# Minus mu as three rows of the score product instead of the sigmoid's bias operand

## What is computed

```python
def _L1_attn_ref(sequence, ln_gamma, ln_beta, Wq, bq, Wk, bk, Wv, bv, Wo, bo, mu):
    ...
    q = _split_heads(x @ Wq.T + bq)
    k = _split_heads(x @ Wk.T + bk)
    v = _split_heads(x @ Wv.T + bv)
    scale = HEAD_DIM ** 0.5
    scores = jnp.einsum('bhqd,bhkd->bhqk', q, k) / scale
    scores = jax.nn.sigmoid(scores - mu) * jnp.exp(scores)
    scores = scores / jnp.sum(scores, axis=-1, keepdims=True)
    out = jnp.einsum('bhqk,bhkd->bhqd', scores, v)
    ...
```

## Time and profile before

| what | value |
|---|---|
| median of 3 runs | 737.53 us |
| the profiled execution, its own time | 736.84 us |
| span in its profile | 735.0 us |
| PE busy | 680.0 us, 93% |
| DVE busy | 459.6 us, 63% |
| ACT busy | 350.2 us, 48% |
| POOL busy | 142.8 us, 19% |
| sigmoid activations (L944) | 64, 67.7 us |
| exp activations of the second attention (L943) | 64, 61.7 us |
| mean granted clock of PE | 0.976 |

### The profile page before, as it was taken

How to read it: one execution, slowest core, us unless ns; L and a number is a source line. 1 busy time by engine, 2 the same in 40 slices (tenths; PEclk the granted TensorE clock), 3 DMA queues, 4 the chain that set the end, 5 groups by cost and what they waited for, 6 DMA issues and landing times.

```text
span 735.0 us, 15948 instructions
## 1 busy us (share of the span) xinstructions
PE 680.0 (93%) x5563; PEld 541.1 (74%) x5563; DVE 459.6 (63%) x1177; ACT 350.2 (48%) x604; POOL 142.8 (19%) x183
## 2 busy tenths in 40 slices
PE   5789999999989999999999999998899999998855
PEld 4668877877768988977878799997576666765433
DVE  3758787887664453256632332333589999978786
ACT  2354455346425211222122212221998999999745
POOL 3010131232223130000000022200434555211000
PEclk9999999999999999999999999999999999999975
DMA  6868133223437466656465657552432244212003
GB/s 175 232 186 250 38 95 102 86 72 86 132 122 248 152 223 231 224 187 218 144 260 195 216 188 230 173 194 58 122 86 61 85 116 115 77 40 58 1 15 101
DMA packets 70311, 102.80 MB, mean 140 GB/s; under 512 B 8400, under 2 KB 57816, under 8 KB 70112
## 3 DMA queue, kind: packets, MB, share of 16 engines
q1 hardware_dynamic: 66848, 93.41, 40.7%
q0 software_dynamic: 3136, 8.40, 3.7%
q10 hardware_dynamic: 256, 0.07, 0.0%
HBM read 64.41 MB, written 12.19 MB: 104 GB/s over the span
## 4 chain that ended last, share of the span: by engine, by line
PE 68%; DVE 16%; issue 5%; ACT 5%; DMA 2%; POOL 1%; DVEq 1%; ACTq 0%; SPq 0%; POOLq 0%
PE psum L2356 17%; PE psum L2303 15%; DVE arena L1487 5%; PE psum L1969 4%; PE psum L2247 3%; PE psum L2261 3%; PE psum L2232 3%; PE psum L2238 2%; PE psum L2293 2%; DVE arena L1342 2%; PE psum L1993 2%; PE psum L1977 1%; PE psum L2331 1%; PE psum L2031 1%; ACT arena L944 1%
## 5 line engine op out<-in xcount | busy, mean ns | idle before, releaser
L2356 PE MATMUL psum<-arena 128*128 (+1 forms) x576 | 130.7, 380 | 1.9 <-DVE arena L1671 1.4
L2303 PE MATMUL psum<-arena 128*128 128x128 f32 x1024 | 120.5, 276 | 1.1 <-issue 1.0
L2303 PEld LDWEIGHTS psum<-arena 128*128 128x128 f32 x1024 | 118.1, 192 | 4.1 <-issue 3.2
L2356 PEld LDWEIGHTS psum<-arena 128*128 128x128 f32 (+1 forms) x576 | 103.2, 184 | 18.8 <-issue 3.2
L978 ACT ACTIVATE arena<-psum,arena 128x128 f32<-128x128 f32 x128 | 36.5, 368 | 148.6 <-DVE arena L1645 106.9
L2247 PE MATMUL psum<-arena 96*128 96x256 bf16 x512 | 74.0, 274 | 6.1 <-ACT arena L943 5.1
L1487 DVE TENSOR_TENSOR arena<-arena 128x1024 f32<-128x1024 f32 x64 | 77.7, 1284 | 0.8 <-ACT arena L943 0.8
L1671 DVE TENSOR_TENSOR arena<-psum,arena 128x256 f32<-128x256 f32 (+1 forms) x40 | 17.0, 424 | 97.7 <-PE psum L2356 80.9
L2247 PEld LDWEIGHTS psum<-arena 96*128 96x128 bf16 x512 | 44.0, 97 | 37.7 <-ACT arena L943 12.3
L944 ACT ACTIVATE arena<-psum,neg_mu 128x1024 f32<-128x1024 f32 x64 | 67.7, 1118 | 3.7 <-PE psum L2247 3.5
L943 ACT ACTIVATE arena<-psum 128x1024 f32<-128x1024 f32 x64 | 61.7, 1036 | 12.9 <-DVE arena L1671 8.5
(11 more groups left out here) (355 smaller groups left out, 1277.9 us busy)
## 6 DMA issues: line engine op xcount, KB each, us to landing
arena<-in_L_ffn_w_dram SPq DMA_DIRECT2D x48, 1024.0 KB, 5.4
arena<-arena SPq DMA_DIRECT2D x192, 128.0 KB, 2.4
yg<-arena SPq DMA_DIRECT2D x36, 128.0 KB, 1.7
arena<-xg SPq DMA_DIRECT2D x32, 128.0 KB, 2.1
out_dram<-arena SPq DMA_DIRECT2D x8, 256.0 KB, 2.1
xg<-zeros SPq DMA_DIRECT2D x9, 128.0 KB, 2.9
arena<-in_x_dram SPq DMA_DIRECT2D x8, 128.0 KB, 2.2
arena<-in_L_ffn_b_dram SPq DMA_DIRECT2D x1, 1024.0 KB, 14.0
```

Source lines behind the costliest of these rows:

```text
L2303: mm = pe.matmul(psum[:, 2 * v + c // HALF, (c % HALF) * P:(c % HALF + 1) * P], w1[:, d, c * P:(c + 1) * P], xtT[:, v, d, :], start=(d == ...
L2356: mm = pe.matmul(y_bank[0:rows], hidT[:, u, c, 0:rows], w2s[:, one(e), c, :].rearrange("p o n -> p (o n)"), start=(c == 0), stop=(c == HC ...
```

## The change

`scores` gets its number of rows as an argument: 96 in the pass of exp, MU_ROWS = 99 in the pass of sigmoid. The three added rows are ones in `stackq1` and, in `stackk1`, three bf16 parts of minus mu, so that the product comes out as s - mu. ACT's sigmoid has no bias operand any more. The rows are filled once:

- DVE, after tile i = 18: eight small instructions, each waited for, split `neg_mu` into three bf16 parts and put part n into partition 96 + n of a column (`mu_part`).
- POOL, between `scale1(1)` and `gather(2)`: a memset of ones and a copy of the column, spread over 4096 elements, both on 3 partitions; a wait at the end for the copy.
- SP, behind the unit loop: two DMAs copy the rows from the stacks of parity 0 to those of parity 1.
- PE waits for the fill before its first pass and for the two DMAs at batch 1.

`scale1` also lost an argument: both its uses now count on one semaphore.

```diff
+MU_ROWS = ROWS + 3
...
+        MU_STEPS, MU_TILE = W8_STEPS + 8, 18
...
+                sp.wait_ge(S["l1_hi"], UNITS)
+                sp.wait_ge(S["set_done"], 5)
+                for stack in (stackq1, stackk1):
+                    sp.dma_start(stack[1][ROWS:MU_ROWS].rearrange("d h t -> d (h t)"),
+                                 stack[0][ROWS:MU_ROWS].rearrange("d h t -> d (h t)")).then_inc(S["mu_in"], 16)
...
+                def shift_rows():
+
+                    pool.wait_ge(S["l1_hi"], SPARE_UNTIL)
+                    pool.wait_ge(S["n_rstd"], 2)
+                    pool.memset(stackq1[0][ROWS:MU_ROWS], 1.0).then_inc(S["set_done"], 1)
+                    pool.wait_ge(S["l2_mm"], SPARE_UNTIL)
+                    pool.wait_ge(S["w8_step"], MU_STEPS)
+                    pool.wait_ge(S["set_done"], 4)
+                    pool.tensor_copy(stackk1[0][ROWS:MU_ROWS].rearrange("p h t -> p (h t)"),
+                                     mu_part[ROWS:MU_ROWS, :].to_broadcast([MU_ROWS - ROWS, HEADS * T])).then_inc(S["set_done"], 1)
+                    pool.wait_ge(S["set_done"], 5)
+
                 for b in range(3):
+                    if b == 2:
+                        shift_rows()
                     gather(b)
...
-                    return act.activation(out, in_, ACT.Sigmoid, bias=neg_mu[:])
+                    return act.activation(out, in_, ACT.Sigmoid)
...
+                def shift_parts():
+
+                    dve.wait_ge(S["wT_done"], WT_STEPS + 3)
+                    chain(dve.tensor_copy(mu_split[:, 0:1], neg_mu[:]))
+                    chain(dve.tensor_tensor(mu_rest[:, 0:1], neg_mu[:], mu_split[:, 0:1], ALU.subtract))
+                    chain(dve.tensor_copy(mu_split[:, 1:2], mu_rest[:, 0:1]))
+                    chain(dve.tensor_tensor(mu_rest[:, 1:2], mu_rest[:, 0:1], mu_split[:, 1:2], ALU.subtract))
+                    chain(dve.tensor_copy(mu_split[:, 2:3], mu_rest[:, 1:2]))
+                    chain(dve.tensor_tensor(mu_part[:], mu_split[:, 0:1], ident[:, ROWS:ROWS + 1], ALU.mult))
+                    for n in range(1, 3):
+                        chain(dve.scalar_tensor_tensor(out=mu_part[:], in0=mu_split[:, n:n + 1], scalar=ident[:, ROWS + n:ROWS + n + 1],
+                                                       in1=mu_part[:], op0=ALU.mult, op1=ALU.add))
...
+                    if i == MU_TILE:
+                        shift_parts()
...
                             if b == 0 and p == 0:
-                                pe.wait_ge(S["set_done"], 3)
+                                pe.wait_ge(S["set_done"], 5)
+                            if b == 1 and p == 0:
+                                pe.wait_ge(S["mu_in"], 2 * 16)
...
-                            scores(b, u, p, S["s1_mm"])
+                            scores(b, u, p, ROWS if u == 0 else MU_ROWS, S["s1_mm"])
...
-                            scores(b, u, p, S["s2_mm"])
+                            scores(b, u, p, MU_ROWS if u == 0 else ROWS, S["s2_mm"])
```

More of the change, by code:

```diff
@@ L203, in tower_kernel @@
         neg_mu = sb("neg_mu", [P, 1], F32)
+        mu_rest = sb("mu_rest", [P, 2], F32)
+        mu_split = sb("mu_split", [P, 3], BF16)
+        mu_part = sb("mu_part", [P, 1], F32)
         ones_row = sb("ones_row", [1, P], F32)
@@ L422, in tower_kernel @@
             s1_mm f1_done s2_mm f2_done prodD n_pv n_oa n_ot1 n_rr n_on n_ot2 n_oT n_wo n_hbo n_h3
-            m_stat m_mv m_eps m_rstd x3_done am_done
+            m_stat m_mv mu_in m_rstd x3_done am_done
             w8_in w8_step w8_mm w8_done q_step am_mm f_y f_ed qz_q fT_mm fT_done f_mm f_o f_back f_out""".split()
@@ L782, in _, with scale1 @@
                 batches(pool, iteration, B + 2)
-                def scale1(b, n, got, s_eps, s_rstd):
+                eps_steps = [0]
+                def scale1(b, n, got, s_rstd):
                     pool.wait_ge(got, QT * (b + 1))
@@ L788, in scale1 @@
                     scale, shift = (1.0 + LN1_EPS, LN_EPS * LN1_EPS) if n == 0 else (1.0, LN_EPS)
-                    pool.tensor_scalar(n_veps[:, n, :], n_mom[:, n, :, 1], scale, shift, ALU.mult, ALU.add).then_inc(s_eps, 1)
-                    pool.wait_ge(s_eps, b + 1)
+                    pool.tensor_scalar(n_veps[:, n, :], n_mom[:, n, :, 1], scale, shift, ALU.mult, ALU.add).then_inc(S["n_eps"], 1)
+                    eps_steps[0] += 1
+                    pool.wait_ge(S["n_eps"], eps_steps[0])
                     pool.tensor_tensor(n_rs[:, n, :], n_veps[:, n, :], half_exp[:], ALU.pow).then_inc(s_rstd, 1)
@@ L825, in iteration @@
                     if stages(b - 2, 0, LAST):
-                        scale1(b - 2, 1, S["m_mv"], S["m_eps"], S["m_rstd"])
+                        scale1(b - 2, 1, S["m_mv"], S["m_rstd"])
                     if stages(b + 2, 3, LAST):
-                        scale1(b + 2, 0, S["n_mv"], S["n_eps"], S["n_rstd"])
+                        scale1(b + 2, 0, S["n_mv"], S["n_rstd"])
                     if stages(b + 1, 1, LAST):
@@ L831, in iteration @@
                         second_part(b + 1, 1, S["n_kr"], S["n_km"])
+                def shift_rows():
[8 more added lines that the diff above has]
+                    pool.wait_ge(S["set_done"], 5)
                 for b in range(3):
+                    if b == 2:
+                        shift_rows()
                     gather(b)
-                    scale1(b, 0, S["n_mv"], S["n_eps"], S["n_rstd"])
+                    scale1(b, 0, S["n_mv"], S["n_rstd"])
                 gather(3)
@@ L1606, in tile_slots @@
                     assert placed[0] == PLACE_STEPS, placed[0]
+                def shift_parts():
[9 more added lines that the diff above has]
+                                                       in1=mu_part[:], op0=ALU.mult, op1=ALU.add))
+                    assert steps[0] == MU_STEPS
                 def weight_maximum():
@@ L2240, in project_token_tile, with scores @@
                     return mm
-                def scores(b, u, p, done):
+                def scores(b, u, p, rows, done):
                     for i in range(2):
@@ L2247, in scores @@
                             mm = pe.matmul(area[p % 2][:, i, kt * T:(kt + 1) * T],
-                                           stackk1[u][0:ROWS, hd, kt * P:(kt + 1) * P], stackq1[u][0:ROWS, hd, :],
+                                           stackk1[u][0:rows, hd, kt * P:(kt + 1) * P], stackq1[u][0:rows, hd, :],
                                            start=True, stop=True)
```

## The result

The change takes **734.98 us** (median of 7 runs, 733.83 to 735.84), the kernel before 737.78 us in the runs beside it: a ratio of 0.9949, 95% interval [0.9928, 0.9971]. Two later comparisons gave 0.9973 [0.9957, 0.9989] and 0.9963 [0.9945, 0.9982]. All 31 runs of the change have a mean of 735.37 us, all 131 of before 737.67: 2.3 us less, with a standard error of 0.25, and three times the 0.7 that was forecast.

A forecast was written before the change was run, and what follows sets the result against it. PE was taken to hold 68% of the chain of waits, ACT 5%. Gains of 0.2 us (first three sigmoid phases) and 0.5 (last), additions at 0, make 737.53 - 0.7 = 736.8 us; range 734.9 to 738.3, 75% for the forecast.

The forecast's parts named there:

- The activations and the additions: Second attention's sigmoids without bias run like exp, 0.7 us less in all; work added on PE, DVE, POOL, SP costs 0.
- each pair of phases: First three sigmoid phases (batches 0/1, 2/3, 4/5): 0.06 us less each by the chain, 0.2 together.
- The last phase: Sigmoid phase of batches 6/7: 0.2 us at PE's last weighing plus 0.27 at three closing sigmoids, about 0.5 less.
- Fills, products of 99 rows, SP's DMAs and both waits: POOL's fills of 6.6 to 8.5 us, PE's longer products, two DMAs and PE's two new waits: each priced at 0.
- The rival that lets every phase gain its full 0.45: ACT sets the pace in its phases: 3.0 us less, 734.5; 12% together with a 6.5 us case.
- The slower rival: POOL's copy takes 10.8 us and holds DVE's eviction, PE's second layer loses 5.6 us: 742.4; 7%.
- the third: Rival: the 82 ns are the sigmoid's own, not the bias column's, so nothing is gained, 737.5; 6%.
- Eight on one element each ... Cost 0: DVE's eight instructions after tile 18 are covered by PE's two layers: cost 0, without cover up to 3.6 us.
- the sum had no term for PE's clock: Adding up of the forecast: 0.2 + 0.5 = 0.7 us less, from the phases of sigmoid only.
- What a measurement can tell: About 0.3%, 2.2 us, is what a measurement of this kernel can tell from no change; 77% for within.

The follow-up runs named there:

- kept busy: Either kernel with idle products (matmuls nobody uses) added where PE waits; everywhere: change 734.11 and 733.78 us, before 734.19 and 734.68 us.
- experiment 1: Kernel before with the sigmoid's bias operand alone taken away, minus mu left out of the result: ratio 0.9985, mean 736.77 us.
- experiment 2: The change with its bias operand put back, so all additions stay and nothing is taken away: ratio to before 1.0005.
- experiment 7: Kernel before without the bias operand and with the change's eight DVE instructions at tile 18, result unused: ratio 0.9975.
- experiments 11 to 13: Seven idle products (unused matmuls) in batch 7, in before: 0.9988; the same in the change: 0.9977; the change with one DVE copy in batch 6: 0.9974.

## Why the prediction was wrong

**The activations and the additions: right.** Sigmoid and exp take the same; each pair of phases is 0.1 us shorter, so three of them 0.37 instead of 0.2 (kept busy profiles: 0.09, 0.16 and 0.12). The last phase gains 0.45 by the faster activations alone (21.21 to 20.76, experiment 1), 0.5 was forecast. Together 0.8, forecast 0.7; experiment 1's runs say 0.9, with an error of 0.4. Fills, products of 99 rows, SP's DMAs and both waits: nothing, as priced (experiment 2). The rival that lets every phase gain its full 0.45 falls with the phases of exp, which became longer, and experiment 1; that its 3.0 us lie near the measured gain is an accident. The slower rival falls with DVE's eviction, which was not held, the third with 1032 ns.

**"Eight on one element each ... Cost 0": the wrong sign.** Where they stand they cost nothing. Behind them, 280 us later, a stall for issue of 0.23 us is gone, which is worth 20.76 - 20.47 = 0.29 us once ACT is fast enough to let it through (experiment 7), and nothing while it isn't (experiment 2: 21.22). The step looked for who waits at tile 18, not for what else a longer program moves.

**The step that failed: the sum had no term for PE's clock.** It set terms of a tenth of a microsecond against one execution, and took PE's speed there as the kernel's own. The rows at 44 and 214 us of that same profile show PE at half its clock, and nobody asked what such a fall is worth, where PE's idle stretches could bring others, or whether the change moves them. In batch 7 five of the six profiles with a last phase of 20.60 us or longer meet one, at 1.5 us; the profile that was read is the sixth, so this cost was invisible there. The change, whose last phase is 0.74 us shorter, met none in three profiles, nor did experiment 7. As an estimate the whole is 0.8 + 0.3 + 1.5 x 5/6 = 2.35 us, and 737.67 - 735.37 = 2.3 were measured. That falls make most of what the sum lacked is shown: with idle products in the gaps, and no fall left, the two kernels are 0.7 us apart instead of 2.3. That the falls which the change is spared are those of batch 7 rests on ten profiles and the estimate from the clock; the times of experiments 11 to 13 don't settle it. The first comparison's 2.8 us lie 0.5 above the mean of all runs, which is luck.

**"What a measurement can tell", 0.3%,** stood for the falls without naming them. Their scatter is a good part of why a ratio here has an interval of 0.0016 to 0.0023 to either side: kept busy, before's runs have a standard deviation of 0.8 us instead of 1.7.

**Open.** Why the same wait of 1.72 us brings a fall in one execution and not in the next, and why a tenth or a few of a microsecond in the last phase's length should decide. The Trainium skill (TensorE: Matmul & The Clock Gate, Part 1: The HAM clock gate) says that the hardware watches PE's activity without regard to when a kernel starts; the two executions of before, alike in their rows and not in their clock, agree with that. Five of six against none of four is few. Where DVE's stall comes from, beyond that the instructions ahead of it move it, was not tried.

A version better than both came out: the change kept busy everywhere, 733.78 us in the mean of 16 runs, 1.6 under the change and 3.9 under before.

## What to carry to other kernels

Before you weigh tenths of a microsecond, list the stretches at a low granted clock, price each (the same instructions at either level), and look at a second execution: what falls there is part of the kernel's time even where the profile at hand lacks it. A change that takes work off ACT can pay as much by shortening or moving PE's idle stretches as by that work itself, and idle products there show how much of a difference is clock. Instructions put into one stage can add or take a stall for issue in a later one, so compare those too.

## What was not expected of the hardware

- The same products behind the same wait ran at 2.4 GHz in one execution and at 1.2 in another (0.60 and 1.06 us for two). Idle products in PE's gaps, 44 in all, took every fall out between 14 and 690 us and 3.2 us off the kernel before.
- Eight small instructions on DVE (0.15 to 0.22 us each) removed a stall of 0.23 us that stood at the same later instruction in all eight profiles of kernels without them.
- DVE's copy of 128x8, one input in SBUF, was held 1.7 us by POOL's cast, and its addition with one input in PSUM not at all.
